# Window attention over images on one core: scores and values' products in 64-row halves, totals in the values' bank, transfers by channel half, another prologue

## The reference

```python
def _gn(v, G=16, eps=1e-5):
    B_, H_, W_, C_ = v.shape
    g = v.reshape(B_, H_, W_, G, C_ // G)
    m = jnp.mean(g, axis=(1, 2, 4), keepdims=True)
    s = jnp.var(g, axis=(1, 2, 4), keepdims=True)
    return ((g - m) / jnp.sqrt(s + eps)).reshape(v.shape)
```

```python
q, k, v = xh @ Wq, xh @ Wk, xh @ Wv        # 224 -> 224
sim = jnp.einsum('bmhid,bmhjd->bmhij', q2 * scale, k2) + pos_emb   # i, j: 16 windows
attn = jax.nn.softmax(sim, axis=-1)
o = jnp.einsum('bmhij,bmhjd->bmhid', attn, v2)
o = o @ Wo + bo
x = x + o
```

## Time and profile before

| | |
|---|---|
| median of three executions | 3,757.5 us |
| profiled execution | 3,759.67 us |
| its span | 3,757.8 us |
| TensorE (PE) busy | 3,678.7 us, 98% |
| VectorE (DVE) busy | 3,038.3 us, 81% |
| ScalarE (ACT) busy | 2,998.7 us, 80% |
| GpSimd (POOL) busy | 2,015.3 us, 54% |
| DMA engines, mean busy share on the kernel's queue | 52.8% |
| mean granted clock of TensorE | 0.999 |

### The profile page before, as it was taken

One profiled execution on the slowest core, in us unless ns is written; L12 is line 12 of the kernel. 1 busy time (PEld: TensorE's weight loads), 2 busy tenths in 40 slices (PEclk: granted clock), 3 DMA queues, 4 the chain that ended last, 5 costly groups with the idle time before them and its releaser, 6 DMA issues.

```text
span 3757.8 us, 134137 instructions
## 1 busy us (share of the span) xinstructions
PE 3678.7 (98%) x51712; PEld 2734.5 (73%) x51712; DVE 3038.3 (81%) x5019; ACT 2998.7 (80%) x5380; POOL 2015.3 (54%) x3207
## 2 busy tenths in 40 slices
PE   4999999999999999999999999999999999999998
PEld 2777777777777777777777777777777777777776
DVE  5888888888888888888888888888888888888875
ACT  5888888888888888888888888888888888888874
POOL 3555555555555555555555555555555555555553
PEclk9999999999999999999999999999999999999999
DMA  3555555555555555555555555555555555555544
GB/s 81 128 139 146 131 137 146 139 132 141 138 141 135 141 144 132 137 140 145 132 138 143 141 131 143 141 137 135 141 144 132 137 139 146 131 139 141 143 119 117
DMA packets 247888, 511.55 MB, mean 136 GB/s; under 512 B 58577, under 2 KB 59025, under 8 KB 247441
## 3 DMA queue, kind: packets, MB, share of 16 engines
q1 hardware_dynamic: 247440, 504.40, 52.8%
HBM read 118.31 MB, written 117.44 MB: 63 GB/s over the span
## 4 chain that ended last, share of the span: by engine, by line
issue 36%; POOL 23%; DVE 15%; ACT 10%; DMA 7%; PE 5%; SPq 3%; POOLq 1%; DVEq 0%; ACTq 0%
POOL sc L661 6%; ACT xn L439 6%; POOL xlo L669 6%; POOL newton L643 5%; DVE part L566 3%; POOL sc L673 3%; DMA out_y<-x_sb 3%; DVE sc L595 3%; DMA p_bd<-pt_f 3%; DVE pt_f L608 2%; SPq L281 2%; DVE x_sb L578 2%; DVE sm L620 2%; ACT ohi L481 2%; POOL rstd L643 2%
## 5 line engine op out<-in xcount | busy, mean ns | idle before, releaser
L661 POOL TENSOR_TENSOR sc<-sc,mx 128x512 f32<-128x512 f32 x512 | 536.5, 1048 | 941.6 <-DVE mx L602 941.6
L439 ACT ACTIVATE xn<-x_sb,norm_add,norm_mul 112x128 f32<-112x128 f32 x2048 | 1020.6, 603 | 5.8 <-POOL norm_add L654 5.8
L673 POOL TENSOR_TENSOR sc<-sc,rs 128x512 f32<-128x512 f32 x512 | 536.4, 1048 | 625.6 <-DVE rs L622 625.2
L306 PE MATMUL ps_out<-ohi,wo_s 128*112 128x256 f16 x4096 | 721.5, 278 | 1.8 <-DVE x_sb L578 1.8
L306 PE MATMUL ps_q<-xhi,wqk 112*128 112x512 f16 x2048 | 611.0, 380 | 12.3 <-POOL xlo L669 11.3
L590 DVE TENSOR_TENSOR olo<-ps_o,ohi 128x512 f16<-128x512 f32 x512 | 353.7, 691 | 321.8 <-ACT ohi L481 305.8
L306 PE MATMUL ps_k<-xhi,wqk 112*128 112x512 f16 x2048 | 609.3, 379 | 0.0
L335 PEld LDWEIGHTS ps_s<-k_bd,q_sb 128*32 128x32 f32 x16384 | 416.0, 109 | 216.3 <-issue 216.3
L347 PE MATMUL ps_o<-p_bd,v_sb 128*32 128x128 f32 x16384 | 542.6, 273 | 19.0 <-DMA p_bd<-pt_f 18.5
L306 PE MATMUL ps_v<-wv_s,xhi 112*128 112x224 f16 x4096 | 560.4, 259 | 0.0
L669 POOL TENSOR_TENSOR xlo<-xn,xhi 112x1024 f16<-112x1024 f32 x256 | 548.6, 2143 | 14.7 <-ACT xhi L450 14.7
(11 more groups left out here) (69 smaller groups left out, 5854.0 us busy)
## 6 DMA issues: line engine op xcount, KB each, us to landing
k_bd<-k_cut SPq DMA_DIRECT2D x1024, 128.0 KB, 3.5
p_bd<-pt_f SPq DMA_DIRECT2D x2048, 64.0 KB, 2.1
x_sb<-in_x SPq DMA_DIRECT2D x128, 896.0 KB, 6.0
out_y<-x_sb SPq DMA_DIRECT2D x128, 896.0 KB, 5.1
stage<-in_L_conv_Wq SPq DMA_DIRECT2D x2, 98.0 KB
stage<-in_L_conv_Wk SPq DMA_DIRECT2D x2, 98.0 KB
stage<-in_L_conv_Wv SPq DMA_DIRECT2D x2, 98.0 KB
stage<-in_L_conv_Wo SPq DMA_DIRECT2D x8, 24.5 KB
```

The source lines that it names most:

```text
L306: last = nc.tensor.matmul(dst, w_parts(a, ch), x_parts(c, ch), start=(n == 0), stop=(n == 3 * chunks - 1))
L439: nc.scalar.activation(xn[:, b % 2, :, c4, :, :, nw].rearrange("p r c q -> p q r c"), x_sb[:, b % XBUFS].rearrange("p ch (nh r w) -> p (ch ...
L661: nc.gpsimd.tensor_tensor(rows, rows, mx[:, t % 2].unsqueeze(2).broadcast_to(by_row), ALU.subtract).then_inc(shifted, 1)
L673: nc.gpsimd.tensor_tensor(rows, rows, rs[:, t % 2].unsqueeze(2).broadcast_to(by_row), ALU.mult).then_inc(probs, 1)
```

## The change

Scores and values' products are made in two halves of 64 rows. `k_bd` and `p_bd` hold two blocks side by side, no longer four, so a matmul has 64 rows and 64 moving columns, and there are 32 of each kind in a step (64 records). The two halves go to two PSUM banks. For the scores this takes the place of the two buffers, so `score(t+1)` now waits for `biased` of step t, where it waited for t-1. The values' products are written so that their reader finds runs of four elements. The bias `pos_sb` is stored for all 512 elements, no longer broadcast.

The totals go into the values' bank `ps_v`. TensorE makes them between q and v, no longer at the end of its step; ScalarE copies them (`keep_means`) between its wait for v and v_sb; VectorE's first statistics operation is gone. TensorE's waits for scores and values' products stand ahead of the last k matmul.

Loads and stores go by channel half, each with semaphores of its own; stores stand at the end of SyncE's step and one step earlier. The first image is loaded ahead of the weights, and the weights are prepared within the first steps (before t = -11, -10 and -4), beside the first images' statistics. The small inputs are loaded from ScalarE's queue.

```diff
-PV_LAG, OUT_LAG, FINAL_LAG, STORE_LAG = 2, 3, 4, 8
+PV_LAG, OUT_LAG, FINAL_LAG, STORE_LAG = 2, 3, 4, 7
...
-        k_bd = sb("k_bd", [128, 2, HG, HPG, HTOK])
+        k_bd = sb("k_bd", [128, 2, HG, 2, HTOK])
...
-        p_bd = sb("p_bd", [128, 2, PAIRS, UNIT * 32])
+        p_bd = sb("p_bd", [128, 2, 2, UNIT * 32])
...
-        pos_sb = sb("pos_sb", [128, HEADS, 2, WIN])
+        pos_sb = sb("pos_sb", [128, 2, T2, HG, 2, 2, WIN])
...
-        ps_s = [ps(f"ps_s{n}", [128, UNIT * 32]) for n in range(2)]
-        ps_o = ps("ps_o", [128, UNIT * 32])
-        ps_tot = ps("ps_tot", [128, 2 * G])
+        ps_s = ps("ps_s", [128, 2, 512])
+        ps_o = ps("ps_o", [128, 2, 512])
+        ps_tot = ps_v[0:CP, 0, C:C + 2 * G]
...
+            load_x(0, 0, 0)
+            load_x(0, 1, 0)
             for kind, w in ((0, wq), (1, wk)):
...
-                b = image_at(t, LOAD_LEAD)
-                if b is not None:
-                    wait(sp, y_stored[b % XBUFS], 16 * (b // XBUFS), i, 16)
...
+                if t > FIRST + 1:
+                    load_x(image_at(t, LOAD_LEAD), 0, i)
+                    load_x(image_at(t, LOAD_LEAD - 1), 1, i)
...
+                store_y(image_at(t, -STORE_LAG), 0, i)
+                store_y(image_at(t, -STORE_LAG - 1), 1, i)
...
+            def total(b, i):
+                if b is None:
+                    return
+                per_image(pe, summed, b, i, 2 * CH)
+                per_image(pe, means, b - 1, i)
+                for ch in range(CH):
+                    last = nc.tensor.matmul(ps_tot, ones[:, :], part[:, b % 2, ch],
+                                            start=(ch == 0), stop=(ch == CH - 1))
+                last.then_inc(totals, 1)
...
-                        col = (t2 * HG + hg) * 128
-                        for pr in range(PAIRS):
-                            tok = ((g % 2) * T2 + t2) * TILE + pr * 32
-                            last = nc.tensor.matmul(
-                                ps_s[g % 2][pr * 32:pr * 32 + 32, col:col + 128].rearrange("p (h j) -> p h j", j=32),
-                                q_sb[:, h % QBUFS, hg, tok:tok + 32],
-                                k_bd[:, h % 2, hg, :, tok:tok + 32], start=True, stop=True)
+                        col = (t2 * HG + hg) * 64
+                        for half in range(2):
+                            rows = slice(half * 64, half * 64 + 64)
+                            for pr in range(PAIRS):
+                                tok = ((g % 2) * T2 + t2) * TILE + pr * 32
+                                last = nc.tensor.matmul(
+                                    ps_s[pr * 32:pr * 32 + 32, half, col:col + 64].rearrange("p (h j) -> p h j", j=32),
+                                    q_sb[rows, h % QBUFS, hg, tok:tok + 32],
+                                    k_bd[rows, h % 2, hg, :, tok:tok + 32], start=True, stop=True)
...
+                                last = nc.tensor.matmul(
+                                    ps_o[h * 32:h * 32 + 32, half, col:col + 64].rearrange("p (n r c) -> p n r c", r=2, c=2),
+                                    v_sb[rows, g % VBUFS, t2, hg * HPG + h, :],
+                                    p_bd[rows, g % 2, :, unit * 32:unit * 32 + 32].rearrange("p r (c n) -> p n r c", c=2),
+                                    start=True, stop=True)
...
+                def attention_waits():
+                    g = t - PV_LAG
+                    if is_step(g):
+                        probs_placed(pe, g, i)
+                        per_step(pe, v_kept, g, i)
+
+                        per_step(pe, o_lo, g - 1, i)
+                    g = t + 1
+                    if is_step(g):
+                        if g % 2 == 0:
+                            keys_placed(pe, g // 2, i)
+                            per_step(pe, q_kept, g + 1, i)
+
+                        per_step(pe, biased, g - 1, i)
...
                     project_qk(u, 0).then_inc(q_done, 1)
                     per_step(pe, v_kept, u - 1, i)
+                    if image_at(t - 1, TOT_LEAD) is not None:
+                        per_image(pe, means, image_at(t - 1, TOT_LEAD), i)
+                    total(image_at(t, TOT_LEAD), i)
                     project_v(u).then_inc(v_done, 1)
                     per_step(pe, k_kept, u - 1, i)
-                    project_qk(u, 1).then_inc(k_done, 1)
...
+                    project_qk(u, 1, attention_waits).then_inc(k_done, 1)
...
-                b = image_at(t, TOT_LEAD)
-                if b is not None:
-                    per_image(pe, summed, b, i, 2 * CH)
-                    wait(pe, stats, STAT_OPS * (b - 1) + 1, i, STAT_OPS * XBUFS)
...
+            def keep_means(b, i):
+
+                if b is None:
+                    return
+                per_image(act, totals, b, i)
+                per_image(act, factors_ready, b - 1, i, 2)
+                wait(act, stats, STAT_OPS * (b - 1) + 2, i, STAT_OPS * XBUFS)
+                nc.scalar.activation(st[:, :], ps_tot, ACT.Copy, scale=1.0 / GROUP_N).then_inc(means, 1)
...
                     per_step(act, v_done, u, i)
+                keep_means(image_at(t, TOT_LEAD), i)
+                if is_step(u):
...
-            rounds(act, step)
+            rounds(act, step, before_12=load_positions, before_4=weights_split)
...
-            rounds(dve, step)
+            rounds(dve, step, before_11=largest_weights, before_10=split_weights)
```

More of the change, by code:

```diff
@@ L141, in build @@
         totals = sem("totals")
+        means = sem("means")
         stats = sem("stats")
@@ L294, in step, with split_product @@
                         p = slice(hd * DP, hd * DP + DP)
[L295 removed]
+                        sp.dma_start(k_bd[p, h % 2, :, hd % 2, :], k_cut[p, h % 2]).then_inc(k_placed[h % 2], 16)
+                store_y(image_at(t, -STORE_LAG), 0, i)
+                store_y(image_at(t, -STORE_LAG - 1), 1, i)
             rounds(sp, step)
[L297 to L298 removed]
+            for ch in range(CH):
+                for s in range(XBUFS):
+                    sp.wait_ge(y_stored[ch][s], 16 * ((B - s + XBUFS - 1) // XBUFS))
         @block.tensor
         def _(pe):
[L302 removed]
+            def split_product(dst, w_parts, x_parts, chunks=CH, waits=None):
                 n = 0
@@ L305, in split_product @@
                     for ch in range(chunks):
+                        if waits is not None and n == 3 * chunks - 1:
+                            waits()
                         last = nc.tensor.matmul(dst, w_parts(a, ch), x_parts(c, ch),
@@ L312, in _, with project_qk @@
             o_parts = (ohi, olo)
-            def project_qk(u, j):
+            def project_qk(u, j, waits=None):
                 h, hg = divmod(u, 2)
@@ L343, in weigh_values @@
                     for hg in range(HG):
-                        for h in range(HPG):
-                            unit = (t2 * HG + hg) * HPG + h
-                            col = (t2 * HG + hg) * 128
-                            last = nc.tensor.matmul(
-                                ps_o[h * 32:h * 32 + 32, col:col + 128].rearrange("p (r j) -> p r j", j=32),
-                                v_sb[:, g % VBUFS, t2, hg * HPG + h, :],
-                                p_bd[:, g % 2, :, unit * 32:unit * 32 + 32], start=True, stop=True)
+                        col = (t2 * HG + hg) * 64
+                        for half in range(2):
+                            rows = slice(half * 64, half * 64 + 64)
+                            for h in range(HPG):
+                                unit = (((h // 2) * T2 + t2) * HG + hg) * 2 + h % 2
+                                last = nc.tensor.matmul(
[3 more added lines that the diff above has]
+                                    start=True, stop=True)
                 return last
@@ L388, in step, with weights_split, load_positions @@
                     last.then_inc(projected, 1)
-                b = image_at(t, TOT_LEAD)
-                if b is not None:
-                    per_image(pe, summed, b, i, 2 * CH)
-                    wait(pe, stats, STAT_OPS * (b - 1) + 1, i, STAT_OPS * XBUFS)
-                    for ch in range(CH):
-                        last = nc.tensor.matmul(ps_tot[0:CP, :], ones[:, :], part[:, b % 2, ch],
-                                                start=(ch == 0), stop=(ch == CH - 1))
-                    last.then_inc(totals, 1)
+            def weights_split():
+                pe.wait_ge(pads_zeroed, 4)
+                pe.wait_ge(w_hi, 3)
+                pe.wait_ge(w_lo, 3)
             pe.wait_ge(zeroed, N_ZEROED)
-            pe.wait_ge(pads_zeroed, 2)
-            pe.wait_ge(w_hi, 3)
-            pe.wait_ge(w_lo, 3)
-            rounds(pe, step)
+            rounds(pe, step, before_4=weights_split)
         @block.scalar
         def _(act):
-            act.wait_ge(w_scaled, 4)
-            for hi, full in ((wqk, wqk_f), (wv_s, wv_f), (wo_s, wo_f)):
-                nc.scalar.activation(hi[:, 0], full, ACT.Copy).then_inc(w_hi, 1)
```

(18 more changed lines are left out.)

209 lines of the change are left out of this document (107 added, 102 removed).

## The result

Four executions of the changed kernel took 4,396.0 to 4,437.63 us, median **4,428.8**, against 3,756.85 of the kernel before (a fourth execution of it is in this median): ratio 1.177, 95% interval 1.171 to 1.183. The forecast was 4,295 in a range of 3,830 to 4,440, so the median lies inside by 11 us. The profiled execution took 4,431.7 us, and its span is 4,429.9.

The account below looks back on a forecast made before the run. TensorE bound the kernel, the ring close behind. From 3,759.7 us, minus 15 for the prologue, plus 128 images times (33.1 - 28.8) us for the totals' wait and low clock, it forecast 4,295 us, range 3,830 to 4,440.

Parts of the forecast that it names:

- the ring: ScalarE, VectorE, GpSimd cycle, ohi to ohi: 7.52 us in steps 0 and 1, 6.54 in 2 and 3, before the change.
- step 0: Of an image's steps 0 to 3, the one forming the totals; forecast to grow from 7.52 to 11.52 us.
- Totals and v: Terms of step 0 after the squares: totals 0.32 us, v to v_sb 1.43, v_sb to ohi 4.56.
- The clock: TensorE's clock falls about half a microsecond after resuming, with most of v in it: 1.0 us an image.
- The halves: Scores and values' products on eight tiles: both phases 1.88 to about 0.96 us, TensorE's step 6.16, gain hidden by the wait.
- the contiguous layout of ps_o ...: cost nothing: In the values' products' output: ohi and olo still read 512 elements, so the new layout costs nothing.
- Prologue: Before the first q: image 0's statistics run beside the weights' transfers and preparation; gain 0 to 20 us, taken as 15.
- A: Rival: TensorE's clock stays at 1.00, 32.1 us an image, 4,170 us; chance 0.20.
- B: Rival: ScalarE catches up, exp waiting for GpSimd no longer than now; image 30.3 us, 3,940 us; chance 0.14.
- C: Rival: squares are ready when TensorE reaches the totals, step 0 keeps 7.52; image 28.1 us, 3,657 us; chance 0.13.
- D: Rival: issuing bounds TensorE at 29 ns a record, both phases 3.76 us; image 38.8 us, 5,025 us; chance 0.06.
- E: Rival: the row halves don't overlap; costs nothing given TensorE's 3 us in hand, so counted within the forecast.

Follow-up runs that it names:

- e2: The kernel before, with only the totals moved behind q and ahead of v, in their own bank: 4,425.3 us, ratio 1.178.
- e1: The changed kernel with VectorE's last squares formed one step earlier, ahead of the totals: 3,917.5 us, ratio 1.042.
- e4: The changed kernel with ten matmuls of 512 columns between q and the totals, filling most of the wait: 4,218.2 us, ratio 1.123.
- e7: e1 with the halved values' products reading their moving side in a row and writing PSUM with a step: 3,951.8 us, ratio 1.052.
- e12: e1 with sums and squares balanced, values' products of 128 rows read and written in row, and loop start two steps later: 3,786.5 us, ratio 1.008.
- e13: The changed kernel with squares early, sums balanced, scores and values' products of 128 rows again, loop start two steps later: 3,763.9 us, ratio 1.001.

## Why the prediction was right

**Direction, cause and place: right.** TensorE waits for VectorE's squares in every image; ScalarE then waits for v; the ring is cut open once. e2 shows it from one side and e1 from the other.

**The ring's terms: right.** Ohi to ohi, mean over steps 40 to 480: step 0 13.02 us, of which 1.44 go in e4 (11.58, forecast 11.52 without the clock); step 1 7.52 (7.52); step 2 6.70 (6.54); step 3 6.98 (6.54). TensorE's wait was shorter than forecast, 2.76 us instead of over 3, since its own steps did not shrink to 6.16; by the forecast's own argument that changes nothing in the ring, which VectorE's squares set.

**Totals and v: right in sum.** From the totals' start to v_sb took 2.06 at the full clock (1,017.01 to 1,019.07), where the forecast had 0.32 + 1.43; from v_sb to ohi 4.15, where it had 4.56. The two misses nearly cancel, which is luck.

**The clock: mechanism right, size wrong.** The forecast took one case for all images, a fall half a microsecond after resuming, and priced the low clock on totals and v alone: 1.0, at most 1.7. Both steps were short. The falls lie from 2.4 us before the totals' start to 1.9 after, and the low clock also slows k and scores, so that v_sb to ohi grows from 4.15 to 5.73 in the image at 1,050. Where it falls it costs 1.7 to 2.9 us; in a quarter of the images it does not fall. That the mean comes near the 1.7 that the forecast had as its highest price is a coincidence.

**The rest of the miss.** An image takes 1.1 us more than forecast by the ring's means. Of this 0.75 went in e4, most of it the clock's, and 0.34 stayed there, nearly all in step 3.

**The halves: mechanism half wrong, size wrong, and hidden.** "If eight overlap as four do, both phases halve, 1.88 to about 0.96" failed: they take 1.73. Scores went to 0.67, close to what 64 starts at 10 ns need. Values' products stayed at 1.06, in part because of the step "the contiguous layout of ps_o ...: cost nothing". The reads of ohi and olo cost nothing, but I looked only at them: the edit turned the read of the moving side into one with a step. With a read in row they would still not be at 0.48 (0.84 in e7's burst, which writes with a step). And the doubled number of records brought pauses that no row of before shows. "The halves' gain, whether full or nil, is hidden here" held for the 1.73: e2, without halves, is 3 us faster than the change. The pauses are not all hidden. Where none falls into them, steps 2 and 3 of the changed kernel take 6.49 and 6.57 us, as in e2 (6.50 and 6.56), which has none; where one does, 6.94 and 7.13.

**Prologue: a little less.** The first q starts at 41.47 us, 9.9 earlier than the earlier trace rows, where I took 15 and looked for it near 36.

**The count: 128 images should have been 125.** The last images have no totals ahead of them while they are worked on, so they keep their old period. By the spans: 125 x 5.48 = 685 more, less 9.9 for the prologue, is 675; measured 672. Against the forecast, which had 128 x 4.3 = 550: 135 more for the images and 5 for the prologue make 4,435; the profiled execution took 4,431.7.

**The rivals.** A (the clock stays, 4,170) is near what e4 builds: 4,218. B: ScalarE caught up a little, 4.15 for 4.56 behind v, nowhere near 1.8. C's mechanism, squares in time, gives 3,917 in e1, not 3,657: it lacked the pauses and VectorE's crowded step 3; what the stepped read in halves costs the whole kernel no run shows, since e7 shortened the burst and lost the time to pauses. D: records of the scores start 10 ns apart. E: the two halves do overlap, since 64 records of scores take 0.67 us for 0.90 before.

## What to carry to other kernels

Before an operation is moved in an in-order engine's program, look for its last producer's time in the same step: a wait of 2.5 us once in four steps, placed ahead of what three other engines live on, cost 18%, of which the clock was a little under a third. Price a low clock on everything that runs in its stretch, not only on what stands right behind the wait. Parts that look free under such a wait show their price only when it is taken away, so a change of several parts is best undone part by part: once the squares were early, a balance of VectorE's steps gave 70 us, the old values' products 98 and the old scores with their two buffers 45, and what was left is 19 us under the kernel before. Count instructions and the order in which the moving side is read, not only elements: splitting matmuls to fill the array gave 0.2 us a step and took more back in pauses.

## What was unexpected in the hardware

- **A stepped read of the moving side nearly doubled an fp32 matmul of 128 rows.** 32 records of 128 x 128 took 1.89 us with the step and 0.98 without. In halves of 64 rows the median burst took 1.14 us with the step on the read and 0.94 with it on the write.
- **TensorE paused with nothing to wait for.** 1.2 to 1.5 us inside bursts and some 2.2 at the loop's jump. Inside the bursts of values' products that came to 83 to 185 us at 128 fp32 records a step (1.7 in e4, which paused behind them instead), with those of the scores to 475 at 192, and to none at 96 or 64, but for one in e12 and one in e13. The same instructions with the loop's start two steps later paused for 24 us where they had paused for 2.4.
- **Starts 10 to 11 ns apart** for fp32 matmuls of 64 rows and 32 columns on eight tiles, moving side read in row, over 64 and 128 records.
- **More work was faster.** Filling the greater part of a wait of some 2.8 us with matmuls took the mean granted clock from 0.941 to 0.996 and saved 211 us, 5%, most of it by the clock.
